# LayerNorm's bias row in a Sobel stage: the add moved from VectorE to GpSimd

## Chip, cores and metric

One core of a Trainium2 chip runs the whole program. The metric is device microseconds of one execution, lower is better. The kernel before was run three times; the profile is of one further execution.

## What is computed

The input x has shape (2, 192, 112, 112), two images of 192 channels. It passes through four layers: windowed attention with an MLP, a Sobel layer, a 7x7 depthwise block with a hidden layer of 768, and a 13x13 depthwise layer. The change is in the Sobel layer:

```python
def _L1_conv_ref(x, fusion_w, fusion_b, ln_w, ln_b):
    edge_x = _depthwise3x3(x, sobel_x, c)
    edge_y = _depthwise3x3(x, sobel_y, c)
    edges = jnp.concatenate([edge_x, edge_y], axis=1)
    fused = jnp.einsum('bchw,oc->bohw', edges, fusion_w) + fusion_b[None, :, None, None]
    mu = jnp.mean(fused, axis=1, keepdims=True)
    var = jnp.mean(jnp.square(fused - mu), axis=1, keepdims=True)
    normed = (fused - mu) * jax.lax.rsqrt(var + EPS)
    normed = normed * ln_w[None, :, None, None] + ln_b[None, :, None, None]
    return x + jax.nn.gelu(normed, approximate=False)
```

`ln_w` and `ln_b` are two rows of 192 numbers, one for each channel. The change touches the addition of `ln_b`.

## The kernel before, in words

The program is a chain of stages with a barrier of all engines between them: attention, MLP with the Sobel layer, depthwise 7x7, hidden layer, response norm, projection, depthwise 13x13. Activations stay in SBUF in a tile X of 128 partitions (pixels) by 196 blocks by 192 channels. Each engine has its own instruction stream, written out by hand, and engines meet only at semaphores.

The MLP and the Sobel layer share one block of streams: the MLP's first, the Sobel layer's behind it. The MLP also leaves two partly summed copies of its output in HBM, `scratch_u` (differences across) and `scratch_v` (sums along), which the Sobel layer reads.

The Sobel layer works in 28 strips (NS) of 8 lines; a strip is 7 blocks (BX) of 128 pixels. For a strip t:

- SyncE loads four pieces (`load`, L888 to L900) into `xu`, `xm`, `xv`; a slot is loaded again when the edge operation that read it is done.
- VectorE makes the edges in four operations: `edges(t, 0)`, the two upper ones of L980 (128 and 64 partitions of 896), and `edges(t, 1)`, the two lower ones of L986. All read two SBUF tensors. They fill one of two buffers of `edge`.
- TensorE waits for all four (L1043 on), puts the bias into PSUM with four matmuls (L1054) and then runs 42 weight loads and matmuls (L1057), six for each block in the profile's count.
- ScalarE squares each block and sums it into `ss` (L1020).
- GpSimd turns the seven sums into reciprocal standard deviations: it adds 1e-5 (L930), then raises to the power -0.5 (L934). The texts call the second one "the power" and its result rstd.
- ScalarE normalizes each of the seven blocks from PSUM into `f` (L1039).
- VectorE multiplies the strip in `f` by the row `ln_w` ("the scaling", L1004) and adds the row `ln_b` ("the bias add", L1006). Both are one operation on 128x1344 elements, with the row as second operand, repeated over the seven blocks (`per_block`, L857). The add waits for the scaling.
- ScalarE takes the gelu of `f` in place (L1029), and VectorE adds it to X ("the residual", L998). SyncE stores the strip of X (L904).

The order on each engine is fixed. In VectorE's turn j (L988 on) stand: upper edges of strip j, residual of strip j-4, scaling and bias add of strip j-3, lower edges of strip j. ScalarE's turn (L1010 on) has the gelu of strip i-4, two squares of strip i-1, the normalizing of strip i-2, and the other five squares. GpSimd's turn had only the two small operations. `f` and `edge` have two buffers each: ScalarE normalizes strip b when the residual of strip b-2 is done (semaphore `added`). The semaphores `scaled` and `affine` tell of the scaling and of the bias add.

The rows `ln_w` and `ln_b` come by two small DMAs that SyncE issues late in the MLP (`load_rows`, L884; semaphore `rloaded`).

```python
            b = t.back(3)
            if b.inside(NS):
                fb = self.f[:, b.buf(2), :, :]
                dve.wait_ge(q["rloaded"], 32)
                dve.wait_ge(q["normed"], b.n * BX + BX)
                nc.vector.tensor_tensor(fb, fb, self.per_block(0), ALU.mult).then_inc(q["scaled"], 1)
                dve.wait_ge(q["scaled"], b.n + 1)
                nc.vector.tensor_tensor(fb, fb, self.per_block(1), ALU.add).then_inc(q["affine"], 1)
```

Two operations of the MLP's streams are read for comparison: GpSimd's copy of a block of 192 channels into X (L1127) and VectorE's operations on 96x896 elements with two SBUF inputs (L1162, L1176, L1178). Two more come from later stages: GpSimd's add of 192 elements in the projection (L1668) and of one element in the hidden layer (L749).

Of the kernel before, what the change touches and what calls it, by code (L numbers as in the profile page):

```python
# [14 lines left out]
ALU = mybir.AluOpType  # L15
# [8 lines left out]
IMG, BY, BX = 2, 14, 7  # L24
# [4 lines left out]
NS = IMG * BY  # L29
# [788 lines left out]
class Sobel:  # L818
# [104 lines left out]
    def gpsimd(self, pool):  # L923
        nc, q = self.nc, self.q
        nc.gpsimd.memset(self.mhalf[:, :], -0.5).then_inc(q["ready"], 1)
        pool.wait_ge(q["ready"], 1)
        for j in range(2, NS + 2):
            b = Step(0, j - 2, NS)
            pool.wait_ge(q["squared"], b.n * BX + BX)
            nc.gpsimd.tensor_scalar(self.ve[:, :], self.ss[:, b.buf(2), :], 1e-5, None, ALU.add).then_inc(q["var_ok"], 1)  # L930
            pool.wait_ge(q["var_ok"], b.n + 1)
            if b.reached(2):
                pool.wait_ge(q["normed"], b.n * BX - BX)
            nc.gpsimd.tensor_tensor(self.rs[:, b.buf(2), :], self.ve[:, :], self.mhalf[:, :], ALU.pow).then_inc(q["rstd"], 1)  # L934

    def centre_weights(self, dve):
        nc, q = self.nc, self.q
# [50 lines left out]
    def vector(self, dve):  # L988
        nc, q, X = self.nc, self.q, self.X
        for j in range(2, NS + self.LAG):  # L990
            t = Step(0, j, NS)
            if t.inside(NS) and t.n > 1:
                self.edges(dve, t, 0)
            c = t.back(4)
            if c.inside(NS):
                dve.wait_ge(q["gelu"], c.n + 1)
                strip = X[:, bass.ds(c.n * BX, BX), :]
                nc.vector.tensor_tensor(strip, strip, self.f[:, c.buf(2), :, :], ALU.add).then_inc(q["added"], 1)  # L998
# [3 lines that stand above are left out]
                dve.wait_ge(q["rloaded"], 32)  # L1002
                dve.wait_ge(q["normed"], b.n * BX + BX)
                nc.vector.tensor_tensor(fb, fb, self.per_block(0), ALU.mult).then_inc(q["scaled"], 1)  # L1004
                dve.wait_ge(q["scaled"], b.n + 1)
                nc.vector.tensor_tensor(fb, fb, self.per_block(1), ALU.add).then_inc(q["affine"], 1)  # L1006
            if t.inside(NS) and t.n > 1:
                self.edges(dve, t, 1)

# [748 lines left out]
```

## Time and profile before

| what | value |
|---|---|
| three runs | 3543.64, 3544.96, 3550.18 us (median 3544.96) |
| the profiled execution's own time | 3545.38 us |
| its span, first to last instruction | 3543.6 us |
| mean granted TensorE clock | 0.984 |
| busy: TensorE / VectorE / ScalarE / GpSimd | 96% / 68% / 51% / 29% |
| Sobel layer, in the span | about 1798 to 2080 us |

Times are in microseconds from the span's start. PE is TensorE, PEld its weight loads, DVE VectorE, ACT ScalarE, POOL GpSimd, SPq SyncE's DMA queue; L1006 is line 1006 of the kernel. In a timeline each line has start, duration, engine, line, operation, output and inputs with shapes, and in brackets how long the engine had stood idle before and what released it. A duration of a VectorE or GpSimd operation runs from its start to its end, so the time in which it is held up after its start is inside it.

### The profile page before, as it was taken

To read this page: it belongs to the slowest core of one execution; us is meant where nothing else is said; L and a number is where in the kernel's file an instruction comes from. 1 tells how busy PE (TensorE), PEld (TensorE's weight loads), DVE (VectorE), ACT (ScalarE), POOL (GpSimd) and SP (SyncE) were. 2 spreads that over 40 slices of the span, in tenths; PEclk is the share of its full clock that TensorE was granted. 3 is DMA by queue.
4 is the path that set the end of the run, shared out by engine and by line. 5 is a ranking of instruction groups with operands and counts; after the bars stand their busy time and mean duration, and the time that the engine had idled before them with its cause. 6 is when DMAs were issued, how large, how long until landed. Compare 5 with 4: busy or idle time off the path is not lost. (4 is left out here: it accounts for less than half of the span.)

```text
span 3543.6 us, 85540 instructions
## 1 busy us (share of the span) xinstructions
PE 3390.3 (96%) x31678; PEld 3275.9 (92%) x31678; DVE 2394.1 (68%) x5939; ACT 1795.8 (51%) x5312; POOL 1022.8 (29%) x1951
## 2 busy tenths in 40 slices
PE   7999999999799999999978869999999899999999
PEld 6888888888699999999978869989999899999999
DVE  5777777777556667676669989979999311135554
ACT  4666666666444444444436656669999100002222
POOL 4333333333244444444423310014444233320000
PEclk9999999999899999999989989999999899999999
DMA  1455576610111212111158855647777788877775
GB/s 36 132 192 196 199 239 234 236 59 24 27 34 47 55 48 54 51 51 51 51 170 263 267 185 188 197 128 197 197 197 197 228 253 253 253 236 226 226 228 174
DMA packets 472784, 556.39 MB, mean 157 GB/s; under 512 B 78259, under 2 KB 331958, under 8 KB 472374
## 3 DMA queue, kind: packets, MB, share of 16 engines
q1 hardware_dynamic: 447030, 531.65, 49.6%
q10 hardware_dynamic: 25344, 19.27, 1.7%
q8 instruction: 258, 4.23, 0.5%
q14 instruction: 152, 1.25, 0.1%
HBM read 392.56 MB, written 271.52 MB: 187 GB/s over the span
## 5 line engine op out<-in xcount | busy, mean ns | idle before, releaser
L1461 PE MATMUL PS<-dw_grid,dw_mats 128*128 128x196 f32 (+1 forms) x3840 | 626.0, 327 | 33.4 <-DVE dw_mats L1393 33.4
L1461 PEld LDWEIGHTS PS<-dw_grid,dw_mats 128*128 128x128 f32 x3840 | 625.2, 192 | 34.0 <-issue 34.0
L1428 ACT ACTIVATE dw_res<-PS,dw_brow 128x196 f32<-128x196 f32 x192 | 81.6, 425 | 695.8 <-PE PS L1461 695.8
L1276 PE MATMUL PS<-mlp_w,mlp_hid 128*128 128x192 f32 x2352 | 414.4, 326 | 0.5 <-ACT mlp_hid L813 0.5
L1389 DVE COPY dw_grid<-X 32x392 f32<-32x392 f32 (+1 forms) x480 | 290.1, 604 | 163.4 <-PE PS L1461 149.0
L1688 PEld LDWEIGHTS PS<-gain,down_hid 128*128 128x128 f32 x2352 | 384.0, 191 | 4.3 <-DMA down_hid<-scratch_hid 4.3
L1688 PE MATMUL PS<-gain,down_hid 128*128 128x192 f32 x2352 | 384.3, 327 | 3.8 <-DMA down_hid<-scratch_hid 3.8
L1276 PEld LDWEIGHTS PS<-mlp_w,mlp_hid 128*128 128x128 f32 x2352 | 378.6, 190 | 0.8 <-ACT mlp_hid L813 0.8
L813 ACT ACTIVATE mlp_hid<-PS,mlp_b 128x256 f32<-128x256 f32 x588 | 247.0, 471 | 111.8 <-PE PS L804 111.8
L1676 DVE TENSOR_TENSOR X<-PS,down_x 128x192 f32<-128x192 f32 x196 | 70.2, 358 | 318.0 <-PE PS L1688 318.0
L813 ACT ACTIVATE hid_hid<-PS,hidw_b 128x256 f32<-128x256 f32 x588 | 240.9, 471 | 37.7 <-PE PS L804 37.7
L535 ACT ACTIVATE att_vbd<-PS 64x96 f32<-64x96 f32 x784 | 195.1, 249 | 110.0 <-PE PS L631 103.1
L543 ACT ACTIVATE att_qk<-PS,att_qbias 128x256 f32<-128x256 f32 x392 | 164.7, 471 | 148.8 <-PE PS L658 148.8
L1127 POOL COPY X<-mlp_x 128x192 f32<-128x192 f32 x196 | 111.4, 568 | 435.6 <-DVE mlp_x L1203 435.2
L1203 DVE TENSOR_TENSOR mlp_x<-PS,X 128x192 f32<-128x192 f32 x196 | 70.2, 358 | 223.2 <-PE PS L1276 142.8
L414 POOL TENSOR_SCALAR att_xn<-att_x,att_mv,att_rs 128x192 f32<-128x192 f32 x196 | 197.8, 1018 | 20.1 <-POOL att_rs L407 20.1
L1057 PE MATMUL PS<-sobel_wf,sobel_edge 128*128 128x192 f32 x1176 | 200.7, 331 | 0.0
L1057 PEld LDWEIGHTS PS<-sobel_wf,sobel_edge 128*128 128x128 f32 x1176 | 195.0, 194 | 0.0
L1668 POOL TENSOR_TENSOR down_x<-down_x,cvec 128x192 f32<-128x192 f32 x196 | 115.8, 591 | 270.4 <-DMA down_x<-scratch_x 270.4
L403 POOL TENSOR_SCALAR att_ve<-att_mv 128x2 f32<-128x2 f32 x98 | 22.5, 229 | 589.4 <-DVE att_mv L446 589.4
L479 DVE TENSOR_REDUCE att_mx<-PS 128x8 f32<-128x512 f32 x196 | 135.6, 692 | 72.4 <-PE PS L647 72.4
L804 PE MATMUL PS<-mlp_ha_hi,mlp_wa_hi 128*128 128x256 f32 x588 | 174.8, 297 | 0.0
(228 smaller groups left out, 9283.2 us busy)
## 6 DMA issues: line engine op xcount, KB each, us to landing
scratch_hid<-hid_hid SPq DMA_DIRECT2D x196, 384.0 KB, 3.8
down_hid<-scratch_hid SPq DMA_DIRECT2D x196, 384.0 KB, 4.2
scratch_wide<-scratch_taps SPq DMA_DIRECT2D x64, 960.0 KB
dw_raw<-scratch_wide SPq DMA_DIRECT2D x96, 640.0 KB, 4.4
scratch_wide<-scratch_taps SPq DMA_DIRECT2D x64, 768.0 KB
dw_raw<-scratch_wide SPq DMA_DIRECT2D x96, 512.0 KB, 3.4
scratch_u<-mlp_u SPq DMA_DIRECT2D x56, 378.0 KB, 3.0
att_x<-in_x SPq DMA_DIRECT2D x196, 96.0 KB, 2.0
```

Of the source, the lines that this page charges most:

```text
L414: nc.gpsimd.tensor_scalar(xn[:, i, :], x[:, t.buf(XR) - 1 + i, :], mv[:, t.buf(4) - 1 + i, 0:1], rs[:, i:i + 1], ALU.subtract, ALU.mult).t ...
L479: nc.vector.reduce_max(mx[:, b.buf(2), :].rearrange("p (h e) -> p h e", e=2), s4, AX.X).then_inc(q["max"], 1)
L535: last = nc.scalar.activation(vbd[64 * e:64 * e + 64, b.buf(4), w, :, e, 0:HD], src, ACT.Identity)
L543: nc.scalar.activation(qk[:, u.buf(2), ch, :], psQK[i], ACT.Identity, bias=qbias[:, ch:ch + 1]).then_inc(q["qk_ready"], 1)
L804: last = nc.tensor.matmul(self.psU[i][:, e * 256:(e + 1) * 256], w[:, m], h, start=(j == 0), stop=(j == len(terms) - 1))
L813: last = nc.scalar.activation(hid[:, m, :], self.psU[i][:, e * 256:(e + 1) * 256], ACT.Gelu, bias=self.b1[:, m:m + 1])
L1057: last = nc.tensor.matmul(self.psF(t, j), self.edge[:, t.buf(2), k, j, :], self.wf[:, k, :], start=False, stop=(k == self.KT - 1 and (j % ...
L1276: last = nc.tensor.matmul(psD[i], hid[:, p.buf(2), m, i * 128:(i + 1) * 128], w2[:, m, :], start=(m == 0), stop=(m == MC - 1))
L1389: last = nc.vector.tensor_copy(dst, src)
L1461: last = nc.tensor.matmul(dst[:, :, ys, :], m, src, start=(i == 0), stop=(i == len(steps) - 1))
L1668: nc.gpsimd.tensor_tensor(x2[:, b.buf(R), :], x2[:, b.buf(R), :], cvec[:, :], ALU.add).then_inc(q["resid"], 1)
L1688: last = nc.tensor.matmul(PS[:, b.buf(R), 0:C], hid[:, b.buf(R), m, :], gain2[:, img, m, :], start=(m == 0), stop=(m == MC - 1))
```

## The change

VectorE no longer does the bias add. GpSimd does it, in its own turn, which is now one turn longer: in turn j it makes rstd for strip j-2, then waits for the scaling of strip j-3 and adds the row to that strip, in place. GpSimd waits once, ahead of its first turn, for the two rows. Operands, shapes and the semaphore `affine`, which ScalarE's gelu waits for, are the same.

```diff
@@ -924,14 +924,21 @@
         nc, q = self.nc, self.q
         nc.gpsimd.memset(self.mhalf[:, :], -0.5).then_inc(q["ready"], 1)
         pool.wait_ge(q["ready"], 1)
-        for j in range(2, NS + 2):
+        pool.wait_ge(q["rloaded"], 32)
+        for j in range(2, NS + 3):
             b = Step(0, j - 2, NS)
-            pool.wait_ge(q["squared"], b.n * BX + BX)
-            nc.gpsimd.tensor_scalar(self.ve[:, :], self.ss[:, b.buf(2), :], 1e-5, None, ALU.add).then_inc(q["var_ok"], 1)
-            pool.wait_ge(q["var_ok"], b.n + 1)
-            if b.reached(2):
-                pool.wait_ge(q["normed"], b.n * BX - BX)
-            nc.gpsimd.tensor_tensor(self.rs[:, b.buf(2), :], self.ve[:, :], self.mhalf[:, :], ALU.pow).then_inc(q["rstd"], 1)
+            if b.inside(NS):
+                pool.wait_ge(q["squared"], b.n * BX + BX)
+                nc.gpsimd.tensor_scalar(self.ve[:, :], self.ss[:, b.buf(2), :], 1e-5, None, ALU.add).then_inc(q["var_ok"], 1)
+                pool.wait_ge(q["var_ok"], b.n + 1)
+                if b.reached(2):
+                    pool.wait_ge(q["normed"], b.n * BX - BX)
+                nc.gpsimd.tensor_tensor(self.rs[:, b.buf(2), :], self.ve[:, :], self.mhalf[:, :], ALU.pow).then_inc(q["rstd"], 1)
+            b = Step(0, j - 3, NS)
+            if b.inside(NS):
+                fb = self.f[:, b.buf(2), :, :]
+                pool.wait_ge(q["scaled"], b.n + 1)
+                nc.gpsimd.tensor_tensor(fb, fb, self.per_block(1), ALU.add).then_inc(q["affine"], 1)
 
     def centre_weights(self, dve):
         nc, q = self.nc, self.q
@@ -1002,8 +1009,6 @@
                 dve.wait_ge(q["rloaded"], 32)
                 dve.wait_ge(q["normed"], b.n * BX + BX)
                 nc.vector.tensor_tensor(fb, fb, self.per_block(0), ALU.mult).then_inc(q["scaled"], 1)
-                dve.wait_ge(q["scaled"], b.n + 1)
-                nc.vector.tensor_tensor(fb, fb, self.per_block(1), ALU.add).then_inc(q["affine"], 1)
             if t.inside(NS) and t.n > 1:
                 self.edges(dve, t, 1)
 
```

## Rows read from the trace of the kernel before

**Rows 1.** The page, part 1: engine, busy us (share of the span), instructions.

```profile
PE 3390.3 (96%) x31678; PEld 3275.9 (92%) x31678; DVE 2394.1 (68%) x5939; ACT 1795.8 (51%) x5312; POOL 1022.8 (29%) x1951
```

**Rows 2.** The table of stretches, first steady one: busy by engine, clock, DMA.

```profile
1850.00:1900.00 50.00, 42.52 (x254) 40.75 (x253) 48.75 (x41) 34.58 (x128) 16.07 (x13) 1.00 0.79 241
```

**Rows 3.** Timeline of VectorE, one strip's loop.

```profile
1908.30 1.08 DVE L980 TENSOR_TENSOR sobel_edge<-sobel_xm 64x896 f32<-64x896 f32 x1
1909.31 1.54 DVE L998 TENSOR_TENSOR X<-X,sobel_f 128x1344 f32<-128x1344 f32 x1
1910.78 1.54 DVE L1004 TENSOR_TENSOR sobel_f<-sobel_f,sobel_row 128x1344 f32<-128x1344 f32 x1
1912.35 1.56 DVE L1006 TENSOR_TENSOR sobel_f<-sobel_f,sobel_row 128x1344 f32<-128x1344 f32 x1
1913.94 1.09 DVE L986 TENSOR_TENSOR sobel_edge<-sobel_xm 64x896 f32<-64x896 f32 x1
1915.06 1.09 DVE L986 TENSOR_TENSOR sobel_edge<-sobel_xv 128x896 f32<-128x896 f32 x1
```

**Rows 4.** Timeline of VectorE, the first and last scaling of the steady stretch.

```profile
1858.10 1.55 DVE L1004 TENSOR_TENSOR sobel_f<-sobel_f,sobel_row 128x1344 f32<-128x1344 f32 x1
...
2051.21 1.54 DVE L1004 TENSOR_TENSOR sobel_f<-sobel_f,sobel_row 128x1344 f32<-128x1344 f32 x1
```

**Rows 5.** Timeline of TensorE: matmuls of one strip, and two waits.

```profile
1863.55 0.88 PE L1054 MATMUL PS<-sobel_bias_r,sobel_ones_r 128*128 128x384 f32 x4 [1.81 <-DVE sobel_edge L986]
...
1908.15 7.01 PE L1057 MATMUL PS<-sobel_wf,sobel_edge 128*128 128x192 f32 x42
1916.21 0.88 PE L1054 MATMUL PS<-sobel_bias_r,sobel_ones_r 128*128 128x384 f32 x4 [1.05 <-DVE sobel_edge L986]
```

**Rows 6.** Views by tile of GpSimd operations: duration ns least/median/most, first and last start.

```profile
L1668 POOL TENSOR_TENSOR down_x<-down_x,cvec x196: 587/591/597, 2781.5 to 3156.0; 128x192 f32<-128x192 f32 x196
...
L749 POOL TENSOR_TENSOR hid_ve<-hid_mv,hid_small x196: 190/192/194, 2356.9 to 2747.9; 128x1 f32<-128x1 f32 x196
...
L1127 POOL COPY X<-mlp_x x196: 344/349/1293, 982.4 to 1795.8; 128x192 f32<-128x192 f32 x196
```

**Rows 7.** GpSimd in the Sobel stage: timeline, then all its powers by tile.

```profile
1906.93 0.56 POOL L930 TENSOR_SCALAR sobel_ve<-sobel_ss 128x7 f32<-128x7 f32 x1 [5.96 <-ACT sobel_sq L1020]
1907.57 2.18 POOL L934 TENSOR_TENSOR sobel_rs<-sobel_ve,sobel_mhalf 128x7 f32<-128x7 f32 x1
...
2064.92 0.25 POOL L930 TENSOR_SCALAR sobel_ve<-sobel_ss 128x7 f32<-128x7 f32 x1 [6.62 <-ACT sobel_sq L1020]
...
L934 POOL TENSOR_TENSOR sobel_rs<-sobel_ve,sobel_mhalf x28: 1510/2177/5112, 1812.5 to 2065.2; 128x7 f32<-128x7 f32 x28
```

**Rows 8.** Timelines in the MLP: two meetings of GpSimd and VectorE; L1162 by tile.

```profile
1041.29 0.34 POOL L1127 COPY X<-mlp_x 128x192 f32<-128x192 f32 x1
...
1041.29 1.29 DVE L1162 TENSOR_TENSOR mlp_u<-mlp_strips 96x896 f32<-96x896 f32 x1 [0.30 <-ACT mlp_strips L1252]
...
1400.77 1.09 DVE L1176 TENSOR_TENSOR mlp_strips<-mlp_strips 96x904 f32<-96x904 f32 x1
...
1401.16 0.91 POOL L1127 COPY X<-mlp_x 128x192 f32<-128x192 f32 x1
...
1401.90 1.11 DVE L1178 TENSOR_TENSOR mlp_strips<-mlp_strips 96x896 f32<-96x896 f32 x1
...
L1162 DVE TENSOR_TENSOR mlp_u<-mlp_strips x56: 1076/1086/1286, 1015.9 to 1807.6; 96x896 f32<-96x896 f32 x56
```

**Rows 9.** Timeline of SyncE's queue: the second row's DMA.

```profile
1808.78 0.77 SPq L886 DMA_DIRECT2D sobel_row<-in_L_conv_ln_b  x1
```

**Rows 10.** Timeline of VectorE in the tail: a bias add.

```profile
2069.14 1.56 DVE L1006 TENSOR_TENSOR sobel_f<-sobel_f,sobel_row 128x1344 f32<-128x1344 f32 x1
```

**Rows 11.** TensorE early in the stage: timeline, and the stretch's row with its clock.

```profile
1818.55 8.95 PE L1057 MATMUL PS<-sobel_wf,sobel_edge 128*128 128x192 f32 x42
...
1815.00:1830.00 15.00, 10.23 (x46) 9.94 (x46) 6.44 (x7) 4.70 (x21) 1.87 (x2) 0.77 0.58 164
```

## The prediction, made before the changed kernel was run

> **What bounds the kernel now.** The stages follow one another behind barriers, so only the Sobel stage can change. The page has VectorE busy 68% of a span of 3543.6 us [rows 1], but that is an average over eight stages with different limits. So I went to the table of stretches next. From 1850 to 1900 us VectorE is busy 48.75 us of 50, TensorE 42.5, ScalarE 34.6, GpSimd 16.1, and the granted clock is 1.00 [rows 2]: in this stage VectorE is the full engine. Its timeline shows the loop of one strip: edge operation, residual, scaling, bias add, two lower edge operations, each starting as the one before ends, then the first upper edge operation of the next strip [rows 3]. From the scaling at 1858.10 to the one at 2051.21 there are 22 strips in 193.1 us, 8.78 us each [rows 4]. TensorE's timeline shows who follows: 7.01 us of matmuls from 1908.15, then 1.05 us of standing until the second lower edge operation is done [rows 5]. So TensorE needs 8.78 - 1.05 = 7.73 us a strip. VectorE sets the pace, with TensorE a microsecond behind it.
>
> **What leaves VectorE.** One add of 128x1344 in each of 28 strips: start to start 1913.94 - 1912.35 = 1.59 us [rows 3]. VectorE keeps 8.78 - 1.59 = 7.19 us a strip. If nothing else happened, TensorE's 7.73 would set the pace.
>
> **What GpSimd gets.** The trace has no GpSimd add of 1344 elements; I bound it. The same operation on 192 elements takes 591 ns (median of 196). Seven of them are 4.14 us, the upper bound, as it pays the fixed part seven times. The same operation on one element takes 192 ns, so the slope is (591 - 192)/191 = 2.09 ns an element and 1344 elements take 0.19 + 1343 x 2.09 = 3.00 us. A copy, with one input, has a slope of (349 - 192)/191 = 0.82 ns, which would give 1.29 us; that is the floor [rows 6]. I take 3.00, since two rows of the very operation give it. GpSimd's queue has room: its two small operations take 0.56 and 2.18 us of 8.78, and it waits 5.96 us before them [rows 7].
>
> **What the two engines do to each other.** This decides the sign, and the stage before has it. At 1041.29 a GpSimd copy of 0.34 us and a VectorE subtraction with both inputs in SBUF start together: the VectorE one takes 1.29 us instead of 1.09. At 1401.16 the copy arrives inside such an operation and takes 0.91 us instead of 0.35, ending 0.21 us behind it [rows 6, 8]. So they exclude each other, whichever comes first. In the Sobel stage every VectorE operation in the loop has both inputs in SBUF. The small GpSimd operations already pay there: the one on seven elements takes 0.56 us beside an edge operation and 0.25 at the end of the stage, with VectorE idle [rows 7]. VectorE loses nothing to them: the edge operation at 1908.30 and the residual at 1909.31 keep their pace beside the power at 1907.57 [rows 3, 7].
> A long add can't hide like that. Of the copy's 0.34 us VectorE lost 0.20 when both started together, so all but 0.15. Where the copy ran between two VectorE operations, the second took 1.11 us instead of 1.09 for 0.21 us of overhang [rows 8], so some 0.19 us lie in what VectorE spends between two operations anyway. The net loss is 3.00 - 0.15 - 0.19 = 2.66 us a strip. Its bounds are nothing (as beside the small ones) and, with the 4.14, 3.80. I take 2.66, from the rows where GpSimd streams a whole row of elements.
> The Trainium skill, "SBUF — State Buffer", section "SBUF: two separate sides", states that the two engines share a port pair by an exclusive lock, that the first to start keeps it for its whole instruction and that the other fully blocks. By that the loss would be the whole 3.00 and the sum 3582, 8 us more. The trace agrees on the exclusion and has a little less on its length (0.20 of 0.34), and I stay with the rows.
>
> **When GpSimd gets its turn.** The scaling releases the add, and VectorE goes straight on to the lower edge operations. A GpSimd request in the middle of an operation was mostly served at its end: the power at 1907.57 takes 2.18 us, 0.67 over the shortest one, and 0.67 later, at 1908.24, is where one edge operation gives way to the next at 1908.30 [rows 3, 7]. So I expect the add between the two lower edge operations or right behind them; either way VectorE's loop is 7.19 + 2.66 = 9.85 us. What waits for the add has time: counted from the scaling's start, the add ends after 1.6 + 1.1 + 2.9 = 5.6 us, the gelu of 1.3 at 6.9, and the residual that wants it comes at 1.6 + 2.1 + 2.7 + 2.0 = 8.4. Queued behind the add on GpSimd is the next strip's rstd, done about 9 us after the scaling. ScalarE's normalize waits for it and takes 2.3; the result is wanted by the matmuls at about 15 and by the next but one scaling at 20. SP's loads wait on edge operations and its stores on residuals, all at a slower pace, so they have more room, not less. The new wait for the two rows at the head of GpSimd's work costs nothing: the second is issued at 1808.78 [rows 9], the first power is at 1812.5 [rows 7] and the landing has those 3.7 us.
>
> **The sum.** A strip costs +2.66 - 1.59 = +1.07 us. VectorE sets the pace from about 1848 (scaling of strip 1) to 2055 (last edge operations); I count 24 strips, +25.7. Before that the loads set it. At the end two adds stand on the chain one behind the other (scaling, add, gelu, residual, scaling, add, gelu, residual) an add now takes 1.56 [rows 10]: 2 x (3.00 - 1.56) = +2.9. TensorE will stand 2.1 us a strip; it stood 1.81 before 1863.55 [rows 5] and the stretch around that kept 1.00 of 2.4 GHz [rows 2], so I charge nothing. In all +28.6. The profiled execution took 3545.4 us, so **3574**. It is 0.4 us over the median of the three runs, which changes nothing.
>
> **Rivals.**
> A. The exclusion doesn't reach this add, or hardly. TensorE then sets the pace at 7.73: -1.05 x 24 + 2.9 = -22, **3523**, faster. For it: the power of 2.18 us ran beside edge operations at full pace. Against it: that one touches seven elements, and the 192-element copies stretched VectorE [rows 8]. It decides where the net loss is under 1.59 us a strip. Chance 0.09.
> B. Half of that: GpSimd lets go between its reads and VectorE loses about 1.33. That is -0.26 x 24 + 2.9 = -3, **3542**, no change. Chance 0.04.
> C. GpSimd is passed over between operations that follow closely. One of its 28 powers took 5.11 us, 3.6 over the shortest [rows 7], longer than any two VectorE operations. If that is the rule, the add starts only when VectorE stops before the residual, which waits for the gelu, which waits for the add: 1.6 + 2.1 + 2.0 + 2.9 + 1.4 + 1.5 = 11.5 us a strip. +2.72 x 24 + 2.9 = +68, **3613**. Chance 0.10.
> D. The add takes 4.14 us: (1.07 + 1.14) x 24 + 2 x 2.58 = +58, **3603**. For it: the row operand is read again for each of seven blocks, which could cost a start each. Chance 0.09.
> E. TensorE's clock falls to 1.2 GHz for part of each strip. Where the mean granted clock was 0.77, the same matmuls took 8.95 us instead of 7.01 [rows 11, 5]; TensorE would need 7.73 x 8.95/7.01 = 9.9 us, as much as VectorE's loop. A few tenths a strip, +5, **3579**; it belongs to the forecast. Together 0.68.
>
> **The numbers.** The forecast's own range is 3556 to 3592. The range that should hold 8 in 10 goes on over D and C and leaves out A and B: 3555 to 3614. About 0.2%, 7 us, can be told from no change. Faster 0.09 (A), same 0.04 (B), slower 0.87.
>
> **What the next profile would show.** If I am right: scalings 9.8 to 10 us apart; 28 GpSimd adds of about 3.0 us, up to 4 where they waited for an edge operation; one edge operation of each strip recorded near 3.9 us instead of 1.09; TensorE standing 2.1 us before the bias matmuls; the other stages as they are. A: VectorE's durations unchanged and TensorE without waits. C: VectorE idle some 3 us before each residual. D: adds of 4 us with nothing in their way. Edge operations that keep 1.09 us beside a running add would prove me wrong at once.

## The result, and the profile after

The changed kernel takes 3577.3 us (median of 4 runs, 3575.9 to 3581.2) against 3545.0 of the kernel before: a ratio of 1.009, 95% interval 1.0073 to 1.0108. It is 32 us slower; 3574 was forecast. The page of its profiled execution:

```profile
span 3575.2 us, 85540 instructions
## 1 busy us (share of the span) xinstructions
PE 3402.0 (95%) x31678; PEld 3288.5 (92%) x31678; DVE 2411.5 (67%) x5911; ACT 1789.6 (50%) x5312; POOL 1199.4 (34%) x1979
```

VectorE's share falls from 68% to 67% and the span grows by 31.6 us: the engine that lost 28 operations of 1.56 us is busy 17 us more [rows 1]. The table of stretches, same columns as [rows 2]:

```profile
1850.00:1900.00 50.00, 42.59 (x237) 41.27 (x236) 47.57 (x30) 29.12 (x110) 48.61 (x16) 0.93 0.77 231
1900.00:1950.00 50.00, 40.06 (x231) 38.73 (x230) 48.71 (x31) 29.11 (x110) 48.60 (x16) 0.97 0.77 233
```

In [rows 2] VectorE was busy 48.8 us of 50 with 41 operations; now it is 47.6 and 48.7 with 30 and 31. GpSimd went from 16 to 48.6 us of 50. Both look full, but a busy time includes the time in which an operation is held up. VectorE's timeline of one strip, to be laid beside [rows 3], tells why:

```profile
1898.51 1.54 DVE L1011 TENSOR_TENSOR sobel_f<-sobel_f,sobel_row 128x1344 f32<-128x1344 f32 x1
1900.09 1.09 DVE L993 TENSOR_TENSOR sobel_edge<-sobel_xm 64x896 f32<-64x896 f32 x1
1901.20 1.09 DVE L993 TENSOR_TENSOR sobel_edge<-sobel_xv 128x896 f32<-128x896 f32 x1
1902.21 3.93 DVE L987 TENSOR_TENSOR sobel_edge<-sobel_xu 128x896 f32<-128x896 f32 x1
1906.07 1.07 DVE L987 TENSOR_TENSOR sobel_edge<-sobel_xm 64x896 f32<-64x896 f32 x1
1907.07 1.54 DVE L1005 TENSOR_TENSOR X<-X,sobel_f 128x1344 f32<-128x1344 f32 x1
1908.54 1.54 DVE L1011 TENSOR_TENSOR sobel_f<-sobel_f,sobel_row 128x1344 f32<-128x1344 f32 x1
```

The first upper edge operation takes 3.93 us; its median before was 1.08. The others keep their durations. From scaling to scaling it is 1908.54 - 1898.51 = 10.03 us, 7.19 of its own and 2.84 more in that one operation. GpSimd's timeline of the same strip shows with what it coincides:

```profile
1896.31 5.12 POOL L936 TENSOR_TENSOR sobel_rs<-sobel_ve,sobel_mhalf 128x7 f32<-128x7 f32 x1
1901.40 3.79 POOL L941 TENSOR_TENSOR sobel_f<-sobel_f,sobel_row 128x1344 f32<-128x1344 f32 x1
1905.39 0.86 POOL L932 TENSOR_SCALAR sobel_ve<-sobel_ss 128x7 f32<-128x7 f32 x1 [0.19 <-ACT sobel_sq L1025]
1906.33 5.12 POOL L936 TENSOR_TENSOR sobel_rs<-sobel_ve,sobel_mhalf 128x7 f32<-128x7 f32 x1
```

The add is asked for at 1901.40 and ends at 1905.19; with the 3.01 us that it takes alone (below) it began at 1902.2, when the lower edge operations were through. The edge operation of 1902.21 ends at 1906.14, 0.95 us behind the add, where it takes 1.08 undisturbed: nearly all of its work comes after the add. The views by tile of the add and of the power give all 28:

```profile
L941 POOL TENSOR_TENSOR sobel_f<-sobel_f,sobel_row x28: 3012/3788/3929, 1837.7 to 2105.2; 128x1344 f32<-128x1344 f32 x28
...
L936 POOL TENSOR_TENSOR sobel_rs<-sobel_ve,sobel_mhalf x28: 1508/5116/5120, 1817.4 to 2093.5; 128x7 f32<-128x7 f32 x28
```

Alone, in the tail, the add takes 3.01 us; 3.00 was worked out. In the loop it takes 3.79, 0.78 of it waiting. And the power, which took 2.18 us before [rows 7], takes 5.12 in 24 of 28 strips. What follows from that is in TensorE's timeline and in one line of ScalarE's:

```profile
1904.58 8.69 PE L1062 MATMUL PS<-sobel_wf,sobel_edge 128*128 128x192 f32 x42
1913.91 0.85 PE L1059 MATMUL PS<-sobel_bias_r,sobel_ones_r 128*128 128x384 f32 x4 [0.65 <-ACT sobel_f L1044]
1914.61 7.01 PE L1062 MATMUL PS<-sobel_wf,sobel_edge 128*128 128x192 f32 x42
```

```profile
1901.46 2.29 ACT L1044 ACTIVATE sobel_f<-PS,sobel_rs 128x192 f32<-128x192 f32 x7 [4.00 <-POOL sobel_rs L936]
```

ScalarE waits 4.00 us for the power. TensorE waits for ScalarE's normalize, not for the edge operations as in [rows 5], and its matmuls take 8.69 us at 1904.58 and 7.01 at 1914.61: the mean granted clock of the stretches is 0.93 and 0.97, so part of the time it runs at 1.2 GHz. VectorE's timeline at both ends of the steady stretch and in the tail:

```profile
1848.38 1.54 DVE L1011 TENSOR_TENSOR sobel_f<-sobel_f,sobel_row 128x1344 f32<-128x1344 f32 x1
...
2078.96 1.54 DVE L1011 TENSOR_TENSOR sobel_f<-sobel_f,sobel_row 128x1344 f32<-128x1344 f32 x1
2096.03 1.55 DVE L1011 TENSOR_TENSOR sobel_f<-sobel_f,sobel_row 128x1344 f32<-128x1344 f32 x1
2103.53 1.55 DVE L1011 TENSOR_TENSOR sobel_f<-sobel_f,sobel_row 128x1344 f32<-128x1344 f32 x1
```

The scaling of strip 1 is at 1848.38 (before: 1848.58, a line of the same view) and that of strip 24 at 2078.96 (2051.21 in [rows 4]): +27.95 us over 23 strips. From there to the last residual the tail takes 30.60 us, before 26.88: +3.72. Together 31.7, the whole difference.

### The profile page after: what moved, and what is told of

It reads as the page before. It is cut to its first block and busy times, and to the rows that moved or that the text cites. A ratio compares the mean times of both kernels' runs of the same rounds, so it can differ in the third digit from the quotient of the medians.

```text
span 3575.2 us, 85540 instructions
## 1 busy us (share of the span) xinstructions
PE 3402.0 (95%) x31678; PEld 3288.5 (92%) x31678; DVE 2411.5 (67%) x5911; ACT 1789.6 (50%) x5312; POOL 1199.4 (34%) x1979
## 5 line engine op out<-in xcount | busy, mean ns | idle before, releaser
L1062 PE MATMUL PS<-sobel_wf,sobel_edge 128*128 128x192 f32 x1176 | 213.5, 345 | 0.0
L1062 PEld LDWEIGHTS PS<-sobel_wf,sobel_edge 128*128 128x128 f32 x1176 | 208.1, 204 | 0.0
```

The lines of the kernel that those rows point to most:

```text
L1062: last = nc.tensor.matmul(self.psF(t, j), self.edge[:, t.buf(2), k, j, :], self.wf[:, k, :], start=False, stop=(k == self.KT - 1 and (j % ...
```

## The experiments

Each kernel was run beside the kernel before on the same chip, where that one took 3549.6 to 3550.3 us (medians over 8 to 13 runs; the first comparison had 3545.0). So times of kernels are compared by their distance from that one, and first of all by their pace. The pace below is the distance from the scaling of strip 4 to that of strip 24 in VectorE's timeline, divided by 20.

| kernel | pace, us a strip | time, us | ratio to before, 95% interval |
|---|---|---|---|
| before / changed | 8.78 / 10.03 | 3545.0 / 3577.3 | 1.009, 1.0073 to 1.0108 |
| add_twice | 11.49 | 3621.8 | 1.0203, 1.0183 to 1.0224 |
| moved_gap | 10.02 | 3585.9 | 1.0102, 1.0081 to 1.0122 |
| copy_more | 9.76 | 3572.3, one run | |
| memset_more | 9.65 | 3574.2, one run | |
| one_input | 9.88 | 3577.1, one run | |
| sum_lower | 8.55 | 3546.1 | 0.9986, 0.9976 to 0.9996 |
| three_of_seven | 9.27 | 3562.1 | 1.0038, 1.0025 to 1.0051 |
| add_left_out | 8.35 | 3536.9 | 0.9962, 0.9948 to 0.9976 |
| left_out_gap | 7.99 | 3522.0 | 0.9924, 0.9909 to 0.9939 |
| half_words | 8.12 | 3530.9 | 0.9947, 0.9930 to 0.9963 |
| half_gap | 7.80 | 3522.0 | 0.9924, 0.9909 to 0.9939 |
| half_gap_xv | 7.70 | 3517.5 | 0.9911, 0.9894 to 0.9927 |

### Is it the exclusion, or GpSimd's full queue?

GpSimd's stretched operations fill 9.8 us of the 10.03, so it could be GpSimd that sets the pace. Two kernels ask. In add_twice VectorE adds too:

```diff
+                dve.wait_ge(q["scaled"], 2 * b.n + 1)
+                nc.vector.tensor_tensor(fb, fb, self.per_block(1), ALU.add).then_inc(q["scaled"], 1)
...
-                pool.wait_ge(q["scaled"], b.n + 1)
+                pool.wait_ge(q["scaled"], 2 * b.n + 2)
```

> VectorE keeps its bias add, and GpSimd then adds the row a second time to the same strip, ahead of the gelu (the row is added twice). Exclusion (the two engines' operations on SBUF can't run together, so the add takes its time from VectorE's loop): VectorE's own 8.78 us a strip plus the 2.84 that an edge operation was stretched by in the changed kernel, 11.6 us a strip, with VectorE busy or held up all the time; some 3545 + 24 x 2.84 + 3 adds of 3 us in the tail = 3622 us. Queue (the new pace of 10.03 us is GpSimd's own, whose operations fill 9.8 us of it, and VectorE merely follows): GpSimd's work is the same as in the changed kernel, so the pace stays near 10.03 us and the time near 3580 us.

Measured: 3621.8 us, 72 over its kernel before (77 expected), at 11.49 us a strip. GpSimd's work is the changed kernel's, and the pace is VectorE's 8.78 plus 2.71. By tile:

```profile
L993 DVE TENSOR_TENSOR sobel_edge<-sobel_xv x28: 1091/3797/3823, 1805.9 to 2122.1; 128x896 f32<-128x896 f32 x28
...
L941 POOL TENSOR_TENSOR sobel_f<-sobel_f,sobel_row x28: 3012/3921/3944, 1845.1 to 2149.3; 128x1344 f32<-128x1344 f32 x28
```

This time the second lower edge operation bears it, 3.80 us instead of 1.09. In moved_gap the power is let in early (why this does so comes below):

```diff
             c = t.back(4)
+            if t.inside(NS):
+                dve.wait_ge(q["edges"], t.n * self.OPS + 2)
             if c.inside(NS):
```

> The changed kernel with the wait of left_out_gap: ahead of the residual VectorE waits for its own second upper edge operation. Exclusion: the power falls from 5.1 to 2.2 us and GpSimd is idle 3 us a strip, and all the same the pace stays at 10.0 to 10.1 us, since VectorE's own operations and the add fill it; 3577 to 3581 us. Queue (GpSimd's stretched power and the rstd behind it set the pace): the pace falls towards 9 us, under 3560.

```profile
L936 POOL TENSOR_TENSOR sobel_rs<-sobel_ve,sobel_mhalf x28: 1507/2177/2302, 1822.7 to 2101.1; 128x7 f32<-128x7 f32 x28
...
1955.60 3.94 POOL L941 TENSOR_TENSOR sobel_f<-sobel_f,sobel_row 128x1344 f32<-128x1344 f32 x1 [2.78 <-DVE sobel_f L1013]
...
1956.68 3.81 DVE L993 TENSOR_TENSOR sobel_edge<-sobel_xv 128x896 f32<-128x896 f32 x1
```

The power takes 2.18 us in the loop and GpSimd waits 2.78 us for the scaling, and the pace is 10.02, unchanged. It is made up otherwise: 7.19 of VectorE's own, 2.72 in the second lower edge operation and 0.1 for the added wait. The time is 36 us over its kernel before, the changed kernel's was 32; the loop isn't longer for it, but it starts later (the scaling of strip 1 is at 1853.74 instead of 1848.38). The queue theory falls twice.

### What excludes what?

copy_more has VectorE add as before and GpSimd copy the strip onto itself, `tensor_copy(fb, fb)` in place of its add.

> VectorE keeps its bias add; GpSimd copies the strip onto itself ahead of the gelu (one input instead of two; the result is unchanged). The 192-element copy takes 349 ns, the one-element operation 192, so 1344 elements take about 1.3 us. Exclusion of anything that reads SBUF: about 1.1 us lost a strip, 9.9 us a strip, about 3577 us, with one edge operation of a strip near 2.2 us. Exclusion of two-input operations alone: 8.78 us a strip and 3545 to 3550 us, edge operations at 1.09 us.

```profile
L941 POOL COPY sobel_f<-sobel_f x28: 1304/2222/2224, 1841.3 to 2102.6; 128x1344 f32<-128x1344 f32 x28
...
L993 DVE TENSOR_TENSOR sobel_edge<-sobel_xv x28: 1092/2079/2081, 1802.4 to 2079.0; 128x896 f32<-128x896 f32 x28
```

A copy of 1.30 us makes the edge operation 0.99 longer, and 9.76 is 8.78 + 0.98 (9.9 was expected, from a loss of 1.1). The time is 23 us over its kernel before, for 32 expected. One input read by GpSimd is enough. memset_more takes the kernel before and clears a buffer without reading:

```diff
+                pool.wait_ge(q["added"], b.n - 1)
+                nc.gpsimd.memset(self.f[:, b.buf(2), :, :], 0.0).then_inc(q["blank"], 1)
+                pool.wait_ge(q["blank"], b.n - 1)
```

> The kernel before, with one more GpSimd operation a strip that reads nothing: it clears the strip's buffer ahead of ScalarE's normalizing, which overwrites it. By the 128x1024 memset of 1.01 us it takes about 1.3 us. If only reading excludes: VectorE's operations keep their durations, 8.78 us a strip, 3545 to 3548 us. If every GpSimd operation on SBUF excludes: 1.1 us lost a strip, 9.9 us a strip, some 3573 us.

The time, 3574.2, reads like the second theory and would have misled. GpSimd's memset, VectorE's scaling beside it, and two lines of the waits from 1860 to 2040 us:

```profile
1957.95 1.22 POOL L935 MEMSET sobel_f<- 128x1344 f32 x1 [2.37 <-DVE X L1001]
...
1957.72 1.55 DVE L1007 TENSOR_TENSOR sobel_f<-sobel_f,sobel_row 128x1344 f32<-128x1344 f32 x1
...
ACT sobel_f L1042 <- POOL sobel_rs L937: 60.9, 19, 3.8
POOL sobel_f L935 <- DVE X L1001: 45.2, 19, 2.6
```

The memset takes 1.22 us inside the 1.55 of a scaling that reads two inputs, and neither is longer for it: its 26 durations are all 1217 to 1227 ns, and no edge operation is over 1.094. What costs time is where I had put it: ahead of the power, behind the residual, so that ScalarE waits for rstd. That is a chain, not exclusion. The expected 3545 to 3548 us left it out. Next, VectorE's side: operations with one input. one_input replaces the two upper edge operations by sums over the same elements.

```diff
-                nc.vector.tensor_tensor(self.in_blocks(t, k, rows), ... , ALU.add).then_inc(q["edges"], 1)
+                    nc.vector.reduce_sum(self.junk[rows, 2 * t.n + i:2 * t.n + i + 1], tile[rows, 0:8, :].rearrange("p r x -> p (r x)"), AX.X).then_inc(q["edges"], 1)
```

> The changed kernel, with the two upper edge operations of strips 2 and on replaced by sums over the same 896 elements, which read one SBUF input instead of two and write one element (those edges are left out). Theory 'the port of the second input': a one-input VectorE operation isn't held up, so the sums keep about 1.0 us beside the add; the add starts behind the lower edge operations and 2 us of its 2.84 lie beside the sums, so VectorE loses about 0.9 us in the residual instead, near 8.1 us a strip, and the time is some 45 us under the changed kernel's. Theory 'any VectorE operation on SBUF': one sum is stretched to 3.8 us and the pace stays at 9.9 to 10.0 us.

The time was 3577.1 (45 us less was expected by the first theory), and not for the second theory's reason:

```profile
1950.08 3.81 DVE L997 TENSOR_TENSOR sobel_edge<-sobel_xv 128x896 f32<-128x896 f32 x1
1953.81 1.07 DVE L991 TENSOR_REDUCE sobel_junk<-sobel_xu 128x1 f32<-128x896 f32 x1
...
1954.08 1.51 POOL L937 TENSOR_TENSOR sobel_rs<-sobel_ve,sobel_mhalf 128x7 f32<-128x7 f32 x1
```

GpSimd was ready sooner, so the add came in between the two lower edge operations, and it is the two-input one at 1950.08 that waited. But the power at 1954.08 ran its undisturbed 1.51 us beside a sum; beside two-input edge operations it takes 2.18 [rows 7]. sum_lower moves the sums to where the add is:

> The changed kernel with the two lower edge operations of strips 2 and on replaced by sums over the same 896 elements, one SBUF input each (those edges are left out). These are the operations that follow the scaling, so the GpSimd add meets them and not the upper ones. Theory 'the second input': the sums keep 1.07 us, the add takes 3.0 us in every strip and some 2.1 us of it lie beside them, the first upper edge operation loses the remaining 0.8: 8.0 us a strip, near 3530 us. Theory 'any VectorE operation on SBUF': a sum is stretched to 3.8 us, 9.9 us a strip, 3577 us.

```profile
L942 POOL TENSOR_TENSOR sobel_f<-sobel_f,sobel_row x28: 3012/3043/3058, 1841.8 to 2073.4; 128x1344 f32<-128x1344 f32 x28
...
L997 DVE TENSOR_REDUCE sobel_junk<-sobel_xm x26: 1082/1082/1085, 1832.0 to 2050.8; 64x1 f32<-64x896 f32 x26
...
1950.60 1.93 DVE L988 TENSOR_TENSOR sobel_edge<-sobel_xu 128x896 f32<-128x896 f32 x1
```

The add takes 3.01 to 3.06 us in all 28 strips and the sums 1.08 to 1.09: side by side, neither waits. The upper edge operation behind them has two inputs, and it is the one that waits for the rest of the add, 1.93 us instead of 1.08. The time is 4 us under its kernel before, where the changed kernel was 32 over. Two strips in three go at 8.03 or 8.04 us, the 8.0 that was expected; in the third, 9.51 us, a power of 5.12 us stood ahead of the add, which came so late that the edge operation took 3.18. The mean is 8.55.

The sums differ from the edge operations in a second way: they write one element, not 896. And a sum isn't every operation with one SBUF input. The trace of the kernel before has rows for both questions. Four lines are from VectorE's and GpSimd's timelines. The first two lie in the projection, where VectorE adds PSUM and one SBUF tensor into X; the next two in the MLP. The last is the view of L1165, a VectorE copy:

```profile
2925.79 0.36 DVE L1676 TENSOR_TENSOR X<-PS,down_x 128x192 f32<-128x192 f32 x1 [1.59 <-PE PS L1688]
2925.85 0.59 POOL L1668 TENSOR_TENSOR down_x<-down_x,cvec 128x192 f32<-128x192 f32 x1 [1.14 <-DMA down_x<-scratch_x]
...
1016.29 0.89 POOL L1127 COPY X<-mlp_x 128x192 f32<-128x192 f32 x1
1016.91 0.35 DVE L1165 COPY mlp_u<-mlp_carry 96x112 f32<-96x112 f32 x1
...
L1165 DVE COPY mlp_u<-mlp_carry x56: 202/208/355, 1016.9 to 1808.6; 96x112 f32<-96x112 f32 x56
```

L1676 reads one SBUF tensor and writes 192 elements on each partition; it takes 0.358 us in all 196 cases, and the GpSimd add beside it its usual 0.59, whichever of the two starts first (at 2913.69 it is the add, with L1676 at 2914.09). So a VectorE operation that writes a whole row isn't held up for that. But the copy of L1165, with one SBUF input, takes 0.35 us in the 16 cases in which a GpSimd copy is under way, and 0.20 or 0.21 in the other 40. It is held up too.

So what is kept apart for certain is a GpSimd operation that reads SBUF and a VectorE one with two SBUF inputs. Of operations with one SBUF input, the sums and L1676 ran free and the copy of L1165 did not; what marks it off, no run here tests. The Trainium skill, "SBUF — State Buffer", section "SBUF: two separate sides", has an exclusive lock for the first pair in just these terms, and names VectorE operations in a 2-port perf mode beside those with two SBUF inputs. On the first pair the trace agrees: a GpSimd copy excludes, a memset doesn't, a VectorE sum isn't excluded. On the length it agrees nearly: 3.01 us of add cost 2.84 or 2.71, 1.30 us of copy 0.99. Whether L1165 is of the second kind, no run here shows.

### Does a split pay?

three_of_seven leaves four blocks to VectorE (`fb[:, 0:4, :]`) and gives GpSimd three.

> GpSimd adds the row to 3 of the strip's 7 blocks and VectorE to the other 4. Exclusion: the GpSimd add of 576 elements takes 0.19 + 576 x 2.09 = 1.39 us alone and costs VectorE that less 0.17, 1.22; VectorE's add of 768 elements about 0.98 from start to start. 7.19 + 0.98 + 1.22 = 9.39 us a strip, between the two kernels, near 3560 us. No exclusion: 8.2 us, about 3531 us.

It came to 3562.1 us, 12 over its kernel before, and 9.27 us a strip, in between as expected. VectorE's add of 768 elements takes 0.958 us and that of 1344 took 1.558, so an element costs it 1.04 ns. The add of 576 elements on GpSimd made an edge operation 1.09 us longer (2.18), that of 1344 2.84: 1.9 and 2.1 ns an element. At these prices no share pays. For the smallest, one block of 192 elements, this is an estimate: GpSimd's 0.59 us less the 0.30 that comes off at best is 0.29 lost, for 0.20 saved.

### What was there to be had?

> No engine adds the bias row (that addition is left out). Both theories: VectorE needs 7.19 us a strip, TensorE 7.73, so TensorE sets the pace: -1.05 us on 23 to 24 strips and two adds of 1.56 us less in the tail, 3517 us. If it comes out so, the GpSimd add costs 60 us in all against a VectorE add of 28, and rival A's gain was there to be had.

Expected were 28 us under the kernel before, measured are 13 (3536.9 against 3549.6), at a pace of 8.35 where TensorE alone needs 7.73. GpSimd's, ScalarE's and TensorE's timelines of add_left_out:

```profile
1950.48 5.11 POOL L934 TENSOR_TENSOR sobel_rs<-sobel_ve,sobel_mhalf 128x7 f32<-128x7 f32 x1
1959.90 1.51 POOL L934 TENSOR_TENSOR sobel_rs<-sobel_ve,sobel_mhalf 128x7 f32<-128x7 f32 x1
...
1955.63 2.29 ACT L1037 ACTIVATE sobel_f<-PS,sobel_rs 128x192 f32<-128x192 f32 x7 [2.66 <-POOL sobel_rs L934]
...
1958.06 0.85 PE L1052 MATMUL PS<-sobel_bias_r,sobel_ones_r 128*128 128x384 f32 x4 [0.99 <-ACT sobel_f L1037]
```

In every second strip the power takes 5.11 us, ScalarE waits 2.66 for it and TensorE 0.99 for ScalarE. The power was asked for inside the second upper edge operation and went ahead only behind the scaling, past two boundaries between VectorE operations. left_out_gap adds the wait shown for moved_gap.

> The kernel without any bias add, which came to 8.35 us a strip instead of the 7.73 of TensorE, with one edit: ahead of the residual VectorE waits for its own second upper edge operation. Theory 'passed over': the missing 0.6 us come from GpSimd's power, which takes 5.1 us in every second strip because VectorE goes from edge to residual to scaling without letting it in, so rstd, normalize and the matmuls are late. Where VectorE waits for its own operation, as the bias add did for the scaling, GpSimd gets in: the power takes 2.2 us or less in every strip, the pace is 7.8 us, and the time about 3520 us. Rival: 8.35 us has another cause (ScalarE's order, or the buffers of f): the time stays at 3537 or gets worse by the wait, 0.1 us a strip.

```profile
L934 POOL TENSOR_TENSOR sobel_rs<-sobel_ve,sobel_mhalf x28: 1507/2172/2425, 1813.0 to 2042.3; 128x7 f32<-128x7 f32 x28
...
1961.58 1.09 DVE L986 TENSOR_TENSOR sobel_edge<-sobel_xv 128x896 f32<-128x896 f32 x1 [1.22 <-DMA sobel_xv<-scratch_v]
```

The power is 2.17 us, at most 2.43, and the time 3522.0, 28 under its kernel before, where add_left_out was 13 under: 15 us for a wait. The pace is 7.99, for 7.8 expected. The second line has a likely cause of the rest to 7.73, a load of xv that comes late: between 1868 and 2030 us VectorE waited for xv 14 times, 10.7 us in all.

### A version that beats both

half_words makes `f` and the row operand bfloat16.

```diff
-        self.f = s.sb("f", [128, 2, BX, C])
+        self.f = s.sb("f", [128, 2, BX, C], mybir.dt.bfloat16)
+        self.row_h = s.sb("row_h", [128, 2, C], mybir.dt.bfloat16)
...
+        nc.vector.tensor_copy(self.row_h[:, :, :], self.row[:, :, :]).then_inc(q["halved"], 1)
```

> The kernel before with the strip buffer f and the row operand in bfloat16: scaling and bias add read and write 16-bit words (this rounds the normalized value to bfloat16; X and all else stay float32). If VectorE does them at double rate, 0.8 us each, its loop is 7.3 us and TensorE's 7.73 sets the pace: 3517 us, or 3535 if the power is passed over. If the rate doesn't change, 3545 us. In any case it would be the add's own cost that goes, with nothing handed to GpSimd.

```profile
L1008 DVE TENSOR_TENSOR sobel_f<-sobel_f,sobel_row_h x28: 840/848/854, 1839.5 to 2059.5; 128x1344 bf16<-128x1344 bf16 x28
L1010 DVE TENSOR_TENSOR sobel_f<-sobel_f,sobel_row_h x28: 857/858/860, 1840.3 to 2060.4; 128x1344 bf16<-128x1344 bf16 x28
```

Scaling and add take 0.85 and 0.86 us instead of 1.54 and 1.56, with all of it on VectorE. The time is 3530.9 us, at a pace of 8.12, and the power takes 4.41 us in about every second strip. half_gap adds the wait; half_gap_xv also gives xv a second buffer in the room that the 16-bit `f` leaves, and loads it a strip earlier.

```diff
-        if i == 3:
-            return 0, t.n, t.n - 1
...
-        self.xv = s.sb("xv", [128, 10, HW])
+        self.xv = [s.sb(name, [128, 10, HW]) for name in ("xv", "xv2")]
...
-                self.load(sp, Step(0, j + 1, NS), range(3))
-            self.load(sp, Step(0, j, NS), (3,))
+                self.load(sp, Step(0, j + 1, NS))
```

> half_words with the wait of left_out_gap: ahead of the residual VectorE waits for its own second upper edge operation. If the power passed over in every second strip is what half_words lacks to TensorE's pace, the power takes 2.3 us at most, the pace goes from 8.1 to 7.8 or 7.9 us and the time to about 3522 us. If loads of xv come late instead, as twice in left_out_gap, it stays near 8.0 and 3526.

> half_gap with a second buffer for the fourth piece of the loads, xv, in the place that the 16-bit f leaves free, and that piece loaded a strip earlier. If the 0.2 to 0.3 us a strip that left_out_gap kept over TensorE's 7.73 were waits for xv, they go: 7.75 us a strip and 3517 us. If not, no change against half_gap.

3522.0 and 3517.5 us. The power and one wait of TensorE in half_gap_xv:

```profile
L932 POOL TENSOR_TENSOR sobel_rs<-sobel_ve,sobel_mhalf x28: 1508/2174/2305, 1814.5 to 2035.8; 128x7 f32<-128x7 f32 x28
...
1958.09 0.88 PE L1057 MATMUL PS<-sobel_bias_r,sobel_ones_r 128*128 128x384 f32 x4 [0.20 <-DVE sobel_edge L984]
```

At 7.70 us a strip TensorE stands 0.20 us or nothing: it is the bound. Against half_gap the intervals overlap, so the time doesn't prove the second buffer; the pace (7.80 to 7.70) speaks for it, and so do VectorE's waits for xv between 1868 and 2030 us: 2.4 us in half_gap, none here. Against the kernel before both are clearly faster, by 28 and 32 us. The price is that the normalized value and the gelu are rounded to bfloat16.

## Why the prediction was right, point by point

- **What bounds the kernel before**: right. VectorE 8.78, TensorE 7.73. In half_gap_xv, with VectorE's loop shorter, the power let in and xv in two buffers, the pace is TensorE's, 7.70; with the add gone and the power let in alone it is 7.99.
- **What GpSimd gets**: 3.00 us worked out from 192 and one element, 3.01 measured. Rival D is out.
- **Exclusion**: the step that decided the sign, and right. Two copies of 0.35 us in the stage before were enough to see it. Rivals A and B are out by the 3.93 us row.
- **Its size**: the net loss was put at 2.66 us; it was 2.84. I took off 0.15 for the end of the operation and 0.19 for what lies between VectorE operations, and held that the place of the add makes no difference. It does: behind the lower edge operations, as here, only 0.17 comes off (3.01 - 2.84), between them, as in add_twice, moved_gap and one_input, 0.30 (3.01 - 2.71). Over 23 strips that is 4.1 us too little. Against it stand 24 strips where there are 23, and a first one that took 9.5 us before already (1848.58 to 1858.10), 1.8 us too much together: the loop came to +27.95 for +25.7. So part of the closeness of 3574 to 3577.3 is luck, two errors that offset. By the Trainium skill, "SBUF — State Buffer", section "SBUF: two separate sides", the loss is the whole instruction; the 3582 that this gives is 5 us too high: measured, the truth lies between.
- **When GpSimd gets its turn**: the add came right behind the lower edge operations, as one of the two places named. But I took it that a request is mostly served at the next boundary and called the one power of 5.11 us rival C's, an exception. It is what happened to the power in 24 of 28 strips. The add itself was never passed over, so C's 3613 didn't come.
- **The slack of what waits behind the add**: wrong for the next strip's rstd. The power ended 12.9 us after the scaling ahead of it (1911.45 - 1898.51), not 9, and TensorE did come to wait for normalize. It cost nothing only because VectorE's loop was longer still, as moved_gap shows, where the power takes 2.18 us and the pace is the same.
- **TensorE's clock** (rival E): it fell in part of the strips, 8.69 us of matmuls against 7.01, and didn't set the pace, so its +5 us didn't come. VectorE did wait for those matmuls in 8 strips, up to 1.00 us, but inside the time that the add holds it up anyway: the edge operation then takes 2.84 to 3.65 us instead of 3.93, and the strip 10.01 to 10.05 us like the others.
- **The tail**: +3.7 us for +2.9. The two adds on the chain cost 3.0, as from 2096.03 to 2103.53, 7.50 us from scaling to scaling where 6.01 stood before; the strips ahead of them, where the edge operations end, another 0.7.

## What to carry to other kernels

Before an elementwise operation is handed to GpSimd, look at what VectorE does meanwhile. If its operations have two SBUF inputs, GpSimd's time isn't beside VectorE's but inside it, and at 2.1 ns an element against 1.04 the move loses. Beside VectorE sums over one SBUF tensor, or where GpSimd only writes (the memset), it ran free here; beside a VectorE copy with one SBUF input it did not, so each kind of neighbour has to be looked up in the trace. And when a small GpSimd operation on a chain is slow in the profile, look whether it is being passed over: one wait on VectorE's side was worth 15 us here.

## What the runs showed that I had not expected

- A GpSimd request isn't always served when the running VectorE operation ends. Asked for inside the second upper edge operation, the power went past two boundaries (edge to residual, residual to scaling) and in at the third, 3.6 us later: 5.11 us against 1.51, within a few ns each time. Asked for inside the first upper one it was served at the next boundary (2.18 us). With the wait for VectorE's own second upper edge operation GpSimd got in there (2.17 or 2.18 us) in every strip of the loop. Why the other boundaries differ, no run tells.
- A GpSimd memset of 1.22 us runs beside a two-input VectorE operation and neither gets longer.
- VectorE's two-input multiply and add of 1344 elements take 0.85 and 0.86 us on bfloat16, 1.54 and 1.56 on float32.
